# Turning the expert loop of a perceiver and mixture-of-experts block: which blocks the loop holds, and what stands behind it

## The chip, the cores and the metric

The kernel runs on one core of a Trainium2 chip. The metric is the device time of one execution in microseconds (us), the median of several runs. A profile is taken of one execution by the hardware profiler. Its times start at the first instruction.

## What is computed

The reference is one layer of three parts, each added to its input, on x of 8 x 64 rows of 512 numbers in float32: cross-attention of the normalised rows over a context of 1601 rows, linear attention with a feed-forward part, and a mixture of experts. The change touches the last alone:

```python
router_logits = x @ w_router                     # 512 rows, 8 experts
top_w, top_i = jax.lax.top_k(router_logits, 2)
top_w = jax.nn.softmax(top_w, axis=-1)
for ei in range(8):
    hmid = jax.nn.silu(x @ w0[ei]) * (x @ w1[ei])     # 512 -> 1024
    out = out + gating[:, ei:ei + 1] * (hmid @ wo[ei])
```

## The kernel before

Every engine has its own program, written out by hand, and they meet at semaphores. The work up to the router is unrolled. The experts are worked off in blocks of sorted rows. An expert with more rows than the 128 of its long block has *short blocks* of 32 rows ahead of it (`short_block`); each expert then has one *long block* of 128 rows (`expert_block`). How many short blocks an expert has is only known when the router has run. VectorE works the numbers out into a small integer tensor `blocks`, which holds for each expert the number of its first block and that of its long one, and every engine reads them into registers with a `value_load` (`expert_blocks`), two for each expert. A `Fori` with these bounds inside an `If` (for there may be no short block) runs the short blocks.

The outer `Fori` runs over experts 0 to 6 and holds the short blocks and the long block of one expert. Expert 7's long block differs (nothing follows it, and it takes part in the final sum), so the code of expert 7, short loop and long block, stands a second time behind the loop.

In a long block TensorE multiplies the gathered rows by the four halves of w0 and w1 (`up`, units 0 to 3, into banks 0 to 3), turns the product of silu and gate (`hidden_transposed`), and multiplies by the two halves of wo (`down_part`, units 4 and 5). Weights are split in two parts, so each product is three matmuls (L1532, L1535, L1536 in `product`). ScalarE copies the high part of the next expert's weights (`split_e`, L777), VectorE subtracts for the low part (L1271). A short block uses the weights unsplit (`strips`, L2013). SP's queue loads the weights of expert e + 1 (L450): unit 0 waits for `raw_free`, which TensorE's first matmul of the long block of e gives, and SP's round begins behind the store of the long block before (L469), which waits for the copy of y (`yb`, L843 on ScalarE). ScalarE's queue fetches the rows of the block after next (L812).

The order of blocks in time is set by the data alone; within a block it is the order of the code, engine by engine.

Of the kernel before, what the change touches and what calls it, by code (L numbers as in the profile page):

```python
# [5 lines left out]
def perceiver_block(nc, ins, out):  # L6
# [22 lines left out]
    E, _, FE = ins["L0_ffn_w0"].shape  # L29
    R = 32  # L30
    OV = 24
    NB = E + OV
# [11 lines left out]
    with ExitStack() as ctx:  # L44
        def sb(name, shape, dt=f32, scope=ctx):
            return scope.enter_context(nc.sbuf_tensor(name, shape, dt))
# [142 lines left out]
        blocks = sb("blocks", [P, 2, E], mybir.dt.int32, moe)  # L189
# [134 lines left out]

        def expert_blocks(engine, e):

            most = NB - 1 if isinstance(e, int) else NB - 2
            return [engine.value_load(blocks[0:1, i, bass.ds(e, 1)], min_val=0, max_val=most) for i in range(2)]

        TB = [bank[0], bank[1], bank[2]]  # L330
        SB = [bank[3], bank[4]]
# [245 lines left out]
        def _(act):  # L577
# [249 lines left out]
            def silu(b, half, n=512):  # L827
                act.wait_ge(unit_done[2 * half], b + 1)
                nc.scalar.activation(sg[half][:, 0:n], bank[2 * half][:, 0:n], ACT.Silu).then_inc(silu_ready, 1)
# [15 lines left out]
            def short_block(b):  # L845

                silu(b, 0, P)
                silu(b, 1, P)
                whole_hidden(b, 0)
                next_rows(b)  # L850
                whole_hidden(b, 1)
                output_copied(b, P)
                act.wait_ge(y_ready, b + 2)
                row = row_of(b) * R
                nc.scalar.dma_start(ys[bass.ds(row, R), :].rearrange("t (q c) -> q t c", q=FULL_R), yb[:, 0:P]).then_inc(y_stored, 16)

            def expert_block(b, e, last=False):

                def split(j):
                    if not last:  # L860
                        split_e(e + 1, j, (unit_done[j], b + 1))

                silu(b, 0)
                if last:
                    act.wait_ge(xg_loaded, 16 * b + 16)
                    act.wait_ge(y_stored, 16 * b + 1)
                    nc.scalar.activation(drained[:, :], mhalf[:, :], ACT.Copy).then_inc(prior_stored, 1)
                split_e(e, 4)
                split_e(e, 5)
                split(0)  # L870
                silu(b, 1)
                upper_hidden(b, 0)
                split(1)
                split(2)
                upper_hidden(b, 1)
                if last:
                    act.wait_ge(rank_done, 3)
                    nc.scalar.activation(in_lastT, bank[7][:, :].rearrange("p (t n) -> p t n", n=P), ACT.Copy).then_inc(gap_exp, 1)
                    act.wait_ge(unit_done[5], b + 1)
                    nc.scalar.activation(y_hi, bank[6][:, :], ACT.Copy).then_inc(y_hi_ready, 1)  # L880
                    return
                next_rows(b)
                split(3)
                output_copied(b, D)
# [4 lines left out]
                first_upper_rows(k)  # L889
            nc.scalar.activation(drained[:, :], mhalf[:, 0:NT], ACT.Silu)  # L890
            act.wait_ge(slots_ready, 5)
            with act.Fori(0, E - 1) as e:
                first_b, last_b = expert_blocks(act, e)
                with act.If(first_b < last_b):
                    with act.Fori(first_b, last_b) as b:
                        short_block(b)
                expert_block(last_b, e)
            first_b, last_b = expert_blocks(act, E - 1)
            with act.If(first_b < last_b):
                with act.Fori(first_b, last_b) as b:  # L900
                    short_block(b)
            expert_block(last_b, E - 1, last=True)

        @block.vector
        def _(dve):
# [111 lines left out]
            last = statistics((2,))  # L1017
# [257 lines left out]
            for n in range(FF // P):  # L1275
# [12 lines left out]
                if n in (1, 2):  # L1288
                    for t in range(NT):
                        last = nc.vector.tensor_tensor(xt[:, t, :], xt[:, t, :], x1n[:, t, :] if n == 1 else b2_bc, ALU.add)  # L1290
# [170 lines left out]
            def short_block(b):  # L1461

                hidden(b, 0, P)
                hidden(b, 1, P)
                lower_rows(b + 1)

            def expert_block(b, e, last=False):

                def split(j):
                    if not last:  # L1470
                        split_e(e + 1, j)

                split_e(e, 2)
                split_e(e, 3)
                hidden(b, 0)
                if last:
                    for t in range(NT):
                        half = nc.vector.tensor_scalar(in_last[:, t, :], lane[:, :], rel[0][:, t:t + 1], None, ALU.is_equal)
                    link(half)
                    for t in range(NT):  # L1480
                        whole = nc.vector.scalar_tensor_tensor(in_last[:, t, :], lane[:, :], rel[1][:, t:t + 1], in_last[:, t, :],
                                                               ALU.is_equal, ALU.add)
                    whole.then_inc(chosen_ready, 1)
                split_e(e, 4)
                split_e(e, 5)
                lower_hidden(b, 0)
                if last:
                    gates_made()
                hidden(b, 1)
                if last:  # L1490
                    gathered_added(0)
                split(0)
                lower_hidden(b, 1)
                if last:
                    return
                lower_rows(b + 1)
                split(1)

            link(nc.vector.tensor_scalar(rel_all[:, :, :], slotf_all[:, :, :], last_start[:, 0:1], None, ALU.add))
            dve.wait_ge(slots_ready, 4)  # L1500
            with dve.Fori(0, E - 1) as e:
                first_b, last_b = expert_blocks(dve, e)
                with dve.If(first_b < last_b):
                    with dve.Fori(first_b, last_b) as b:
                        short_block(b)
                expert_block(last_b, e)
            first_b, last_b = expert_blocks(dve, E - 1)
            with dve.If(first_b < last_b):
                with dve.Fori(first_b, last_b) as b:
                    short_block(b)  # L1510
            expert_block(last_b, E - 1, last=True)

            def last_added(t):

# [12 lines left out]
        def _(pe):  # L1527
# [505 lines left out]
            def short_block(b, e):  # L2033

                pe.wait_ge(xgT_lo_ready, b + KD)
                for j in range(3):
                    short_up(e, j)
                short_transposed(b, 0)
                short_up(e, 3)
                rows_transposed(b + 1)  # L2040
                short_transposed(b, 1)
                pe.wait_ge(y_ready, b + 1)
                short_down(b, e, 0)
                short_down(b, e, 1)

            def expert_block(b, e, last=False):

                pe.wait_ge(xgT_lo_ready, b + KD)
                for j in range(3):
                    up(e, j)  # L2050
                hidden_transposed(b, 0)
                up(e, 3)
                pe.wait_ge(y_ready, b + 1)
                down_ready(b, e, 0)
                down_part(0, [0])
                hidden_transposed(b, 1)
                if last:
                    pe.wait_ge(chosen_ready, NT + 1)
                    for t in range(NT):
                        mm = nc.tensor.transpose(bank[7][:, t * P:(t + 1) * P], in_last[:, t, :], ident[:, :])  # L2060
                    mm.then_inc(rank_done, 1)
                else:
                    rows_transposed(b + 1)
                down_part(0, [1, 2, 3]).then_inc(unit_done[4], 1)
                down_ready(b, e, 1)
                down_part(1, [0, 1, 2, 3]).then_inc(unit_done[5], 1)

            pe.wait_ge(slots_ready, 4)
            with pe.Fori(0, E - 1) as e:
                first_b, last_b = expert_blocks(pe, e)  # L2070
                with pe.If(first_b < last_b):
                    with pe.Fori(first_b, last_b) as b:
                        short_block(b, e)
                expert_block(last_b, e)
            first_b, last_b = expert_blocks(pe, E - 1)
            with pe.If(first_b < last_b):
                with pe.Fori(first_b, last_b) as b:
                    short_block(b, E - 1)
            expert_block(last_b, E - 1, last=True)
            pe.wait_ge(gap_exp, 2)  # L2080
            pe.wait_ge(y_lo_ready, 1)
            for t in range(NT):
# [20 lines left out]
```

## Time and profile before

| | us |
|---|---|
| median of 3 runs | 662.53 (661.16 to 662.87) |
| profiled execution | 661.3 |
| its span, first to last instruction | 659.5 |
| TensorE busy in it | 620.6 |
| VectorE, ScalarE, GpSimd busy | 429.6, 369.9, 206.7 |
| experts, first block to end of last | 438 to 650 |

The profiled execution is compared with the median with its own time, 661.3, not with its span. Busy times are sums over instructions; register, branch and load instructions of a queue count as none of it and are found by their source line (engine names with a q, as PEldq for TensorE's queue). A matmul's listed duration overlaps the next one's, so the pitch of a row of matmuls is read from their starts.

### The profile page before, as it was taken

The numbers are of one execution on the slowest core, as the hardware profiler recorded it, in microseconds if no ns is written. First come the engines' busy times: TensorE is split into PE (matmuls) and PEld (weight loads), VectorE is DVE, ScalarE is ACT, GpSimd is POOL, SyncE is SP. The second block draws the span as 40 slices with busy tenths as digits, with TensorE's granted clock in tenths as the row PEclk, the third lists the DMA queues.
The fourth block names the chain that finished last, engine by engine and source line by source line (L and its number), as shares of the span: only waits on it lengthen the run. The fifth ranks groups of instructions, "written<-read, shape, count | busy, mean of one in ns | idle before, by whom it ended". The sixth has DMA issues, their size and how long they took to land.

```text
span 659.5 us, 12277 instructions
## 1 busy us (share of the span) xinstructions
PE 620.6 (94%) x4593; PEld 503.2 (76%) x4594; DVE 429.6 (65%) x726; ACT 369.9 (56%) x556; POOL 206.7 (31%) x162
## 2 busy tenths in 40 slices
PE   8989999999989999979999999979998999999686
PEld 7867888888867888857788888867776777777464
DVE  7775766657677355666876335746951859768856
ACT  4589998979964344430152224236762747767531
POOL 4159986978893033341000000450000000000023
PEclk9999999999999999999999999979999999999897
DMA  8515544443132612299993232036971969969805
GB/s 322 220 65 199 201 146 151 168 145 128 40 121 82 194 64 96 67 362 393 401 330 108 73 118 65 0 145 237 337 278 39 330 212 339 380 234 336 295 18 173
DMA packets 56576, 125.54 MB, mean 190 GB/s; under 512 B 5200, under 2 KB 5968, under 8 KB 53464
## 3 DMA queue, kind: packets, MB, share of 16 engines
q1 hardware_dynamic: 52592, 117.00, 49.6%
q0 software_dynamic: 1280, 4.20, 1.9%
q10 hardware_dynamic: 2664, 3.80, 1.8%
q8 instruction: 26, 0.43, 0.3%
q14 instruction: 14, 0.11, 0.1%
HBM read 102.83 MB, written 22.15 MB: 190 GB/s over the span
## 4 chain that ended last, share of the span: by engine, by line
PE 71%; DMA 6%; ACT 6%; DVE 5%; issue 5%; POOL 4%; ACTq 2%; SPq 1%; POOLq 0%; DVEq 0%
PE bank L1532 15%; PE bank L1536 14%; PE bank L1535 14%; PE bank L1548 5%; DMA w_raw<-in_L_ffn_w_dram 4%; PE bank L2013 4%; PE bank L1599 3%; POOL nat_lo L505 3%; PE bank L1600 2%; PE bank L1567 2%; PE bank L1568 2%; ACT nat_hi L620 1%; POOL yt L573 1%; PE bank L1775 1%; PE bank L1584 1%
## 5 line engine op out<-in xcount | busy, mean ns | idle before, releaser
L505 POOL TENSOR_TENSOR nat_lo<-raw,nat_hi 128x512 fp32r<-128x512 f32 x104 | 136.2, 1343 | 41.9 <-ACT nat_hi L620 41.7
L925 DVE TENSOR_TENSOR ct_lo<-bank,ct_hi 128x512 fp32r<-128x512 f32 x96 | 65.9, 689 | 33.3 <-ACT ct_hi L587 32.6
L573 POOL DMA_INDIRECT yt<-slots_y,slot_all x8 | 9.4, 1170 | 200.4 <-DVE e_lo L1271 198.2
L620 ACT ACTIVATE nat_hi<-raw 128x512 fp32r<-128x512 f32 x104 | 64.7, 631 | 0.0
L587 ACT ACTIVATE ct_hi<-bank 128x512 fp32r<-128x512 f32 x96 | 57.0, 596 | 9.0 <-PE bank L1548 6.8
L1548 PE MATMUL bank<-ident,raw 128*128 128x128 f32 x384 | 57.7, 273 | 0.3
L1548 PEld LDWEIGHTS bank<-ident,raw 128*128 128x128 f32 x384 | 46.7, 140 | 12.8 <-issue 0.9
L1532 PE MATMUL bank<-w_hi,turned 128*128 128x512 f32 x128 | 51.7, 404 | 4.7 <-issue 4.6
L1532 PE MATMUL bank<-turned,w_hi 128*128 128x512 f32 (+1 forms) x144 | 53.3, 370 | 1.4 <-DVE turned L1076 1.4
L1271 DVE TENSOR_TENSOR e_lo<-e_raw,e_hi 128x2048 fp32r<-128x2048 f32 x24 | 54.1, 2284 | 0.0
L1536 PE MATMUL bank<-turned,w_lo 128*128 128x512 f32 (+1 forms) x144 | 52.8, 367 | 0.0
L1271 DVE TENSOR_TENSOR w_lo<-w_raw,w_hi 128x2048 fp32r<-128x2048 f32 (+1 forms) x24 | 52.3, 2195 | 0.7 <-ACT w_hi L777 0.7
L1535 PE MATMUL bank<-turned,w_hi 128*128 128x512 f32 (+1 forms) x144 | 52.7, 366 | 0.0
L1438 DVE TENSOR_TENSOR hm<-bank,vectors 128x512 f32<-128x512 f32 (+1 forms) x28 | 14.6, 520 | 57.5 <-PE bank L1536 25.7
L1536 PE MATMUL bank<-w_hi,turned 128*128 128x512 f32 x128 | 50.6, 396 | 0.0
L1535 PE MATMUL bank<-w_lo,turned 128*128 128x512 f32 x128 | 50.6, 396 | 0.0
L1599 PE MATMUL bank<-nat_hi,pT 128*128 128x512 f32 x104 | 48.6, 467 | 1.6 <-POOL nat_lo L505 1.1
L777 ACT ACTIVATE w_hi<-w_raw 128x2048 fp32r<-128x2048 f32 x24 | 45.7, 1917 | 4.3 <-DMA w_raw<-in_L_ffn_w_dram 4.3
L777 ACT ACTIVATE e_hi<-e_raw 128x2048 fp32r<-128x2048 f32 x24 | 45.1, 1913 | 1.2 <-issue 1.2
L527 POOL TENSOR_TENSOR w_lo<-w_raw,w_hi 128x2048 fp32r<-128x2048 f32 x6 | 27.6, 4604 | 56.1 <-ACT w_hi L674 56.1
L1532 PE MATMUL bank<-e_hi,turned 128*128 128x512 f32 x96 | 40.9, 426 | 4.2 <-DVE turned L1442 4.1
L1600 PE MATMUL bank<-nat_lo,pT 128*128 128x512 f32 x104 | 40.9, 393 | 0.0
(292 smaller groups left out, 1448.9 us busy)
## 6 DMA issues: line engine op xcount, KB each, us to landing
raw<-in_ctx_dram SPq DMA_DIRECT2D x24, 1024.0 KB, 4.9
w_raw<-in_L_ffn_w_dram SPq DMA_DIRECT2D x24, 1024.0 KB, 7.7
e_raw<-in_L_ffn_wo_dram SPq DMA_DIRECT2D x16, 1024.0 KB, 9.4
w_raw<-in_L_attn_w_dram SPq DMA_DIRECT2D x8, 1024.0 KB, 5.9
slots_x<-zeros SPq DMA_DIRECT2D x1, 8192.0 KB, 28.0
slots_y<-zeros SPq DMA_DIRECT2D x1, 8192.0 KB, 32.9
e_raw<-in_L_ffn_w_dram SPq DMA_DIRECT2D x8, 1024.0 KB, 11.4
vectors<-slots_x ACTq DMA_DIRECT2D x13, 256.0 KB, 5.6
```

What stands on the lines that cost most here:

```text
L505: nc.gpsimd.tensor_tensor(nat_lo[:, j, :], raw[b % 2][:, j, :], nat_hi[:, j, :].bitcast(f32), ALU.subtract).then_inc(nat_lo_ready, 1)
L587: nc.scalar.activation(ct_hi[:, n % CR, :], src, ACT.Copy).then_inc(t_hi, 1)
L620: nc.scalar.activation(nat_hi[:, j, :], raw[b % 2][:, j, :], ACT.Copy).then_inc(nat_hi_ready, 1)
L777: nc.scalar.activation(e_hi[j][:, :, :], e_raw[j][:, :, :], ACT.Copy).then_inc(e_hi_ready[j], 1)
L925: nc.vector.tensor_tensor(ct_lo[:, n % CR, :], src, ct_hi[:, n % CR, :].bitcast(f32), ALU.subtract).then_inc(t_lo, 1)
L1271: low = nc.vector.tensor_tensor(e_lo[j][:, rows_, :], e_raw[j][:, rows_, :], e_hi[j][:, rows_, :].bitcast(f32), ALU.subtract)
L1532: mm = nc.tensor.matmul(dst, lh, rh, start=first and k == 0, stop=False)
L1535: nc.tensor.matmul(dst, lh, rl, start=False, stop=False)
L1536: mm = nc.tensor.matmul(dst, ll, rh, start=False, stop=last and k == n - 1)
L1548: mm = nc.tensor.transpose(TB[n % 3][:, i * P:(i + 1) * P], raw[b % 2][:, CH * (g // CH) + i, (g % CH) * P:(g % CH + 1) * P], ident[:, :])
L1599: nc.tensor.matmul(value_bank(b)[:, :], pT[:, j, :], nat_hi[:, j, :], start=j == 0, stop=False)
L1600: nc.tensor.matmul(value_bank(b)[:, :], pT[:, j, :], nat_lo[:, j, :], start=False, stop=j == NKT - 1).then_inc(v_step, 1)
```

## The change

The outer loop now holds the long block of expert e and then the short blocks of expert e + 1. The short blocks of expert 0 stand ahead of the loop, and expert 7's long block stands directly behind it. The same is done on ScalarE, VectorE and TensorE; SP's loop is as before. The numbers of the short blocks' bounds are still loaded by `expert_blocks` (two loads), the number of the long block by the new `full_block` (one load), so there are three loads in a round instead of two. The diff is shown for TensorE; ScalarE's and VectorE's read the same.

```diff
@@
         def expert_blocks(engine, e):
 
+            return [engine.value_load(blocks[0:1, i, bass.ds(e, 1)], min_val=0, max_val=NB - 1) for i in range(2)]
+
+        def full_block(engine, e):
+
             most = NB - 1 if isinstance(e, int) else NB - 2
-            return [engine.value_load(blocks[0:1, i, bass.ds(e, 1)], min_val=0, max_val=most) for i in range(2)]
+            return engine.value_load(blocks[0:1, 1, bass.ds(e, 1)], min_val=0, max_val=most)
@@
             pe.wait_ge(slots_ready, 4)
+            first_b, last_b = expert_blocks(pe, 0)
+            with pe.If(first_b < last_b):
+                with pe.Fori(first_b, last_b) as b:
+                    short_block(b, 0)
             with pe.Fori(0, E - 1) as e:
-                first_b, last_b = expert_blocks(pe, e)
+                expert_block(full_block(pe, e), e)
+                first_b, last_b = expert_blocks(pe, e + 1)
                 with pe.If(first_b < last_b):
                     with pe.Fori(first_b, last_b) as b:
-                        short_block(b, e)
-                expert_block(last_b, e)
-            first_b, last_b = expert_blocks(pe, E - 1)
-            with pe.If(first_b < last_b):
-                with pe.Fori(first_b, last_b) as b:
-                    short_block(b, E - 1)
-            expert_block(last_b, E - 1, last=True)
+                        short_block(b, e + 1)
+            expert_block(full_block(pe, E - 1), E - 1, last=True)
```

What follows are rows of the program in the order in which it stands, not in which it runs; a taken branch leaves them. First TensorE before, from the last matmuls in the loop to the first of the last block (L2069 is the outer loop, L328 the loads, L2076 and L2077 the If and the inner loop; L2013 are matmuls of short blocks, of which there are more rows than the first shown).

```order
L1535 MATMUL bank<-e_lo,turned 128x512
L1536 MATMUL bank<-e_hi,turned 128x512
L2069 REGISTER_ALU
L2069 COMPARE_AND_BRANCH
L328 TENSOR_LOAD blocks
L328 ISA x2
L328 TENSOR_LOAD blocks
L328 ISA x2
L2076 COMPARE_AND_BRANCH
L2077 UNCONDITIONAL_BRANCH
L2077 ISA
L2013 MATMUL bank<-w_raw,in_last 32x128 x48
```

The same place of TensorE after, the end of a long block, which is now in the middle of the loop (L327 the two loads of `expert_blocks`, L2080 and L2081 the If and the inner loop).

```order
L1539 MATMUL bank<-e_lo,turned 128x512
L1540 MATMUL bank<-e_hi,turned 128x512
L327 ISA
L327 TENSOR_LOAD blocks
L327 ISA x3
L327 TENSOR_LOAD blocks
L327 ISA x2
L2080 COMPARE_AND_BRANCH
L2081 UNCONDITIONAL_BRANCH
L2081 ISA
L2024 REGISTER_ALU
L2017 MATMUL bank<-w_raw,in_last 32x128 x32
```

So the outer loop's branch no longer stands between a long block and the If behind it; the If and the short block's code follow the same matmuls in both. Next TensorE between the end of a short block's code in the loop and the long block behind it, before.

```order
L2013 MATMUL bank<-e_raw,in_last 32x128 x32
L2072 REGISTER_ALU
L2072 COMPARE_AND_BRANCH
L2071 UNCONDITIONAL_BRANCH
L2048 REGISTER_ALU
L1990 REGISTER_ALU
L1532 MATMUL bank<-w_hi,turned 128x512
```

And after, where the outer loop (L2077) turns behind the short blocks; what stands below its branch is the last block of expert 7, and the loop's start has the same load (L332, `full_block`) ahead of its long block.

```order
L2017 MATMUL bank<-e_raw,in_last 32x128 x32
L2081 REGISTER_ALU
L2081 COMPARE_AND_BRANCH
L2080 UNCONDITIONAL_BRANCH
L2077 REGISTER_ALU
L2077 COMPARE_AND_BRANCH
L332 TENSOR_LOAD blocks
L332 ISA x2
L2052 REGISTER_ALU
L1536 MATMUL bank<-w_hi,turned 128x512
```

Between a short block and a long one there now stand the outer loop's branch and one load; behind the loop no short block is left.

## Rows read from the trace of the kernel before

**Rows 1.** The page: busy share of TensorE; instruction packets of its queue, count and MB.

```profile
PE 620.6 (94%) x4593; PEld 503.2 (76%) x4594; DVE 429.6 (65%) x726; ACT 369.9 (56%) x556; POOL 206.7 (31%) x162
...
q8 instruction: 26, 0.43, 0.3%
```

**Rows 2.** Busy time by stretch, experts; (x) counts instructions.

```profile
core 0: us, PE busy (x) PEld busy (x) DVE busy (x) ACT busy (x) POOL busy (x), PEclk, DMA share, GB/s
...
468.00:488.00 20.00, 19.15 (x95) 14.80 (x97) 16.79 (x12) 14.36 (x13) 0.00 (x0) 1.00 0.94 345
...
512.00:530.00 18.00, 18.00 (x83) 14.36 (x84) 14.88 (x11) 13.95 (x13) 0.00 (x0) 1.00 0.92 341
530.00:538.00 8.00, 7.55 (x201) 6.00 (x200) 2.72 (x4) 2.49 (x8) 0.00 (x0) 1.00 0.38 126
```

**Rows 3.** The chain of waits, 600 to 626: start, us, what.

```profile
603.57 0.45 SPq L450
...
604.27 9.91 DMA w_raw<-in_L_ffn_w_dram
```

**Rows 4.** Timeline of TensorE, 483 to 489.

```profile
484.86 0.48 PE L1532 MATMUL bank<-e_hi,turned 128*128 128x512 f32 x1 [0.85 <-DVE turned L1442]
```

**Rows 5.** Timeline of TensorE at the loop's exit, 620 to 630.5.

```profile
620.11 0.40 PE L1536 MATMUL bank<-e_hi,turned 128*128 128x512 f32 x1
625.10 0.77 PE L1532 MATMUL bank<-w_hi,turned 128*128 128x512 f32 x1 [4.59 <-issue]
...
629.49 0.40 PE L1535 MATMUL bank<-w_lo,turned 128*128 128x512 f32 x1
629.72 0.40 PE L1536 MATMUL bank<-w_hi,turned 128*128 128x512 f32 x1
```

**Rows 6.** Source line L2076: ns minimum/median/maximum, first and last start.

```profile
L2076 PEldq COMPARE_BRANCH  x1: 5722/5722/5722, 619.1 to 619.1; - x1
```

**Rows 7.** Source line L2071, the If in the loop.

```profile
L2071 PEldq COMPARE_BRANCH  x7: 80/105/218, 437.5 to 600.1; - x7
```

**Rows 8.** DMA queues, 622.3 to 623.6.

```profile
q8 instruction: 1, 0.02, 5.3%
```

**Rows 9.** DMA queues, 444.9 to 446.

```profile
q8 instruction: 1, 0.02, 5.2%
```

**Rows 10.** DMA queues, 450.6 to 452.

```profile
q8 instruction: 1, 0.02, 4.3%
```

**Rows 11.** DMA queues, 452 to 622, the whole list.

```profile
q1 hardware_dynamic: 23006, 45.56, 72.8%
q10 hardware_dynamic: 2520, 3.54, 6.5%
q14 instruction: 2, 0.02, 0.0%
```

**Rows 12.** Busy time by stretch at the exit; the third figure from the end is TensorE's granted clock.

```profile
620.50:622.60 2.10, 0.01 (x1) 0.00 (x0) 2.10 (x2) 0.60 (x1) 0.00 (x0) 1.00 0.87 313
622.60:629.50 6.90, 4.40 (x11) 3.48 (x12) 1.98 (x1) 0.00 (x0) 0.00 (x0) 0.51 0.07 25
```

**Rows 13.** Timeline of VectorE, 617 to 633.

```profile
622.30 2.28 DVE L1271 TENSOR_TENSOR e_lo<-e_raw,e_hi 128x2048 fp32r<-128x2048 f32 x1
632.91 0.69 DVE L1438 TENSOR_TENSOR hm<-bank,vectors 128x512 f32<-128x512 f32 x1 [8.32 <-PE bank L1536]
```

**Rows 14.** Source line L328, the loads, 485.2 to 487.

```profile
L328 PEldq TENSOR_LOAD <-blocks x2: 300/304/307, 485.4 to 486.2; - x2
```

**Rows 15.** Source line L2069, the outer loop's branch, 484 to 486.5.

```profile
L2069 PEldq COMPARE_BRANCH  x1: 217/217/217, 485.0 to 485.0; - x1
L2069 PEldq FUSED_REGOPS  x1: 50/50/50, 485.3 to 485.3; - x1
```

**Rows 16.** Source line L2072, the inner loop's branch, 510 to 512.5.

```profile
L2072 PEldq COMPARE_BRANCH  x1: 76/76/76, 511.2 to 511.2; - x1
```

**Rows 17.** Timeline of TensorE's weight loads, 511.4 to 512.

```profile
511.87 0.19 PEld L1532 LDWEIGHTS bank<-w_hi,turned 128*128 128x128 f32 x1 [0.20 <-issue]
```

More of the change, by code:

```diff
@@ L891, in _ @@
             act.wait_ge(slots_ready, 5)
+            first_b, last_b = expert_blocks(act, 0)
+            with act.If(first_b < last_b):
+                with act.Fori(first_b, last_b) as b:
+                    short_block(b)
             with act.Fori(0, E - 1) as e:
-                first_b, last_b = expert_blocks(act, e)
+                expert_block(full_block(act, e), e)
+                first_b, last_b = expert_blocks(act, e + 1)
                 with act.If(first_b < last_b):
@@ L896, in _ @@
                         short_block(b)
-                expert_block(last_b, e)
[L898 to L901, printed above, removed]
-            expert_block(last_b, E - 1, last=True)
+            expert_block(full_block(act, E - 1), E - 1, last=True)
         @block.vector
@@ L1500, in _ @@
             dve.wait_ge(slots_ready, 4)
+            first_b, last_b = expert_blocks(dve, 0)
+            with dve.If(first_b < last_b):
+                with dve.Fori(first_b, last_b) as b:
+                    short_block(b)
             with dve.Fori(0, E - 1) as e:
-                first_b, last_b = expert_blocks(dve, e)
+                expert_block(full_block(dve, e), e)
+                first_b, last_b = expert_blocks(dve, e + 1)
                 with dve.If(first_b < last_b):
@@ L1505, in _ @@
                         short_block(b)
[L1506 to L1511, printed above, removed]
+            expert_block(full_block(dve, E - 1), E - 1, last=True)
             def last_added(t):
@@ L2068, in _ @@
             pe.wait_ge(slots_ready, 4)
+            first_b, last_b = expert_blocks(pe, 0)
+            with pe.If(first_b < last_b):
+                with pe.Fori(first_b, last_b) as b:
+                    short_block(b, 0)
             with pe.Fori(0, E - 1) as e:
-                first_b, last_b = expert_blocks(pe, e)
+                expert_block(full_block(pe, e), e)
+                first_b, last_b = expert_blocks(pe, e + 1)
                 with pe.If(first_b < last_b):
                     with pe.Fori(first_b, last_b) as b:
-                        short_block(b, e)
-                expert_block(last_b, e)
-            first_b, last_b = expert_blocks(pe, E - 1)
-            with pe.If(first_b < last_b):
-                with pe.Fori(first_b, last_b) as b:
-                    short_block(b, E - 1)
-            expert_block(last_b, E - 1, last=True)
+                        short_block(b, e + 1)
+            expert_block(full_block(pe, E - 1), E - 1, last=True)
             pe.wait_ge(gap_exp, 2)
```

## The prediction

> **What bounds the kernel now.** I read first the page: TensorE is busy for 620.6 of 659.5 us, no other engine for more than 430 [rows 1]. Then a table of the expert part by stretch, to see whether that also holds there. It does: in the long blocks that follow a short one (450 to 468, 512 to 530, 538 to 556) TensorE is busy 18.0 of 18 us, with some 84 matmuls, and a short block is some 200 matmuls in 8 us [rows 2]. So whatever makes TensorE late there is paid in full. The table also shows the order of the blocks, which the data fix: expert 0 has one short block, 1 none, 2 three, 3 one, 4 none, 5 one, 6 and 7 none.
>
> Two places are not full. Ahead of the long blocks of experts 2 and 3 nothing is lost, but the long blocks that follow a long one directly (468 to 488, 556 to 575, 601 to 620.5) take 0.6 to 0.85 us more. The chain of waits runs there through the copy of y, SP's issue and a weight transfer of 9.9 us [rows 3], and TensorE stands 0.85 us in the first of them [rows 4]. The other place is the way out of the loop. The last matmul of expert 6 starts at 620.11, the first of the last block at 625.10, with 4.59 us idle that no engine released [rows 5]. The queue's own rows say what it did: the branch of the If at L2076, which jumps over the static copy of the short block, began at 619.1 and took 5.72 us [rows 6], where the If in the loop takes 0.08 to 0.22 [rows 7]. Inside those 5.72 us an instruction packet of the 16 KB kind was moved, between 622.3 and 623.6 [rows 8]. So this is code that was not there when it was jumped to.
>
> When is code fetched otherwise? 26 such packets carry TensorE's program [rows 1]. The run executed 4593 matmuls with as many weight loads; without the repeats of the loop (five short blocks of some 400 instructions, six long ones of 168) and with the short copy that never ran this leaves about 6,580 different ones, an estimate of 253 in a packet. One was moved at 444.9 to 446, in the middle of the first short block, and the next at 450.6 to 452, just as the first long block had begun [rows 9, 10]: about 253 instructions apart, so a packet comes each time TensorE's queue walks over a boundary, and it is the one after that in which it now is. From 452 to 622 none came, only two of the other engines' small ones [rows 11]: the loop's 600 instructions stay. At 450.7 the queue had therefore a boundary just behind it: its own packet held the long block and the loop's end, the packet ahead the first 253 instructions after that, and the last block starts some 590 after the start of the long one, in the third packet. That is why the jump missed.
>
> **The change, part by part.** In code order nothing moves: before it is short, long, short, long with the first pair as the loop, after it is the same four pieces with the middle pair as the loop. The matmuls, copies, transfers and their order in time are the same on every engine. Three things change: which jumps are taken, how many values are loaded per round (three instead of two), and where the loop turns.
>
> *(a) The last block.* It now stands right behind the loop's end, and TensorE's queue gets there by the loop's own tail. If that code is there, the 4.59 us go. With them goes what the clock lost: the granted clock was 0.51 from 622.6 to 629.5, where the stretch before shows 1.00 [rows 12], so the ten matmuls from 625.10 to 629.49 took 4.39 us where ten at full clock take 2.33 (0.23 each) [rows 5], a loss of 2.06 us. VectorE was ready: its weight splits ended at 624.6 and it then waited 8.32 us for TensorE [rows 13], so all behind it moves along. Sum: -6.65 us.
>
> *(b) The jump over the short block, now inside the loop.* After the long block of expert 0 come two loads and the If; expert 1 has no short block, so the branch jumps over the block's 400 instructions to the loop's end. That is the same jump as the one at L2076 before, from the same place in the code to the same place, and it is taken at 467 with the packet of 450.6 as the last one fetched [rows 10]. I expect the same miss there. It costs the 4.59 us, plus what now stands behind the branch and not ahead of it: the loop's branch (from 485.0 to 485.3, 0.3) [rows 15] and one load. The loop's two loads start at 485.4 and 486.2, 0.76 us apart with their address and check [rows 14]. That gives 5.6 us idle. The clock: it fell 2.1 us after TensorE stopped and stayed down 6.9 [rows 12]; with 1.1 us more of standing still, 3.4 us are run at half speed, a loss of 1.6. Against it, the 0.85 us of waiting in this block [rows 4] vanish, since the transfers are released by TensorE's start while the clock slows only TensorE. Sum: +6.35 us.
>
> *(c) The third load at other turns.* It is free where TensorE's own queued matmuls cover it. After a short block they do not: the inner branch is decided at 511.2, the next weight load starts at 511.87, and it takes only 0.3 us of queue work to get there [rows 16, 17]. After the change the loop's branch (0.3) and a load (0.76), followed by two register operations (0.2), stand between: the weight load comes at 512.64, 0.77 us late. Three times (experts 2, 3, 5): 2.3 us. Expert 0's long block is entered from above, a load without a taken branch: 0.5 us. The first loads of all have no loop set-up in front: -0.2. At the skips ahead of experts 4 and 6 the next block may start up to 0.76 late, but these are the blocks whose end the weight transfer decides, and that starts from the y copy, not from TensorE [rows 3]; their 0.6 to 0.85 us of waiting cover it: 0. At the exit the third load leaves about 0.1. If the cover were gone, 1.5 more. Sum: +2.7 us.
>
> On ScalarE, VectorE and SP the added load is 0.65 to 0.8 us, ahead of work that waits for TensorE anyhow (VectorE 8.32 us at the extreme [rows 13]): 0. Their short blocks are three operations on VectorE and nine on ScalarE, so no jump of theirs goes far.
>
> Sum: -6.65 + 6.35 + 2.7 = +2.4 us on the profiled execution's 661.3 (span 659.5 and 1.8 around it), 663.7. The median of the runs is 662.5 (661.2 to 662.9), 1.2 higher, so I say **665.0 us**.
>
> Bounds of what the trace doesn't show: from the packet's start at 622.3 to the first matmul at 625.10 lie 2.8 us that any miss has; the 3.2 from the branch to the packet may be shorter where the transfers leave room. They left little at the exit (share 0.87 at 620.5 to 622.6 [rows 12]), and the jump at 467 falls in a stretch with 0.94 [rows 2], so I take the whole 4.59; 1.8 less if not. The clock's loss lies between 0 (no fall) and 2.1; (c) between 1.0 and 4.2. Together: 661 to 668.
>
> The Trainium skill has a rule against this change, in "Runtime: NRT & Kernel Launch", section "Instruction fetch mechanics": a taken branch whose target is outside the current two pages of instructions forces a fetch, and there is no cache beyond them. This trace has the forced fetch, and contradicts the two pages: the loop's 600 instructions are more than two packets of 253 and turned six times without a fetch [rows 11]. By the page the loop after, which also touches the jump's target, would fetch at every round; the same page gives TensorE room for 2048 instructions, by which it would not. No row here holds more than four packets at once.
>
> **The rivals.**
> 1. *The target is there: no miss in the loop.* For it: the packet ahead could be the right one if the boundary lay later than I count. Against: the target is 400 instructions on, more than one packet, and the jump over the same distance missed [rows 6]. Time: 662.5 - 6.65 + 2.7 = 658.6 us. This ends on the other side. It decides itself by one thing: whether the packet that holds the loop's tail is moved by TensorE's walk before 467.
> 2. *The back jump misses too.* A forced fetch may drop what was held, and the loop's start, which lies close to a boundary by the time of its packet [rows 10], would be fetched anew. Nothing in the trace before speaks to it, since it never jumps back after a miss. Another 4.6 to 5.7 us: 670.
> 3. *The loop no longer fits.* It now touches four packets and the one ahead. If four is the limit, each of seven rounds pays at least 4.6 us: 695 or more. For it: no row shows five held. Against: nothing shows a limit either. The two-page rule of the Trainium skill named above is this rival.
> 4. *All hidden.* The load's 0.77 us after short blocks vanish in some slack and the miss is a us or two shorter, while the transfers are less crowded: 661 to 663.
>
> **How the numbers follow.** Moved stall as summed 0.66 (own range 662.5 to 668); rival 4 0.12; rivals 1, 2 and 3 0.08, 0.08, 0.06. The likeliest is 665.0. The range 661.0 to 670.5 leaves out rivals 1 and 3 and the tails. A measurement of this kernel tells 0.3%, 2.0 us, from no change; the sum of 2.4 is close to that, so of the 0.66 I give a third part below it or just at it: slower 0.57, same 0.32, faster 0.11.
>
> **What the profile after would show.** The branch of the If in TensorE's loop with a longest time of some 5.7 us, at 467; an instruction packet at about 470.5 and one at 473.5, and none at 622; TensorE idle 5.6 us at 468.8 without a releaser, and at 620 less than 0.3. The granted clock at half around 471 to 478. Long blocks after short ones starting 0.7 to 0.8 us after the last short matmul's usual gap. I am wrong if the idle time at 468.8 is missing (rival 1), if a second one follows it directly (rival 2) or returns at each round (rival 3), and wrong in (c) if the long blocks after short ones start without delay.

## The result: 0.36% slower, 664.4 us

20 runs of each on the same chips: the changed kernel 664.38 us in the median (662.90 to 666.20, and one execution of 868.8 at a granted clock of 0.65, which the ratio leaves out), the kernel before 662.49 (660.07 to 664.19). The ratio is 1.0036, with a 95% interval of 1.0026 to 1.0046: 2.4 us slower (662.5 x 0.0036), between 1.7 and 3.0. The profiled execution has a span of 663.2 us where before it had 659.5.

The page of the changed kernel has the same work and the same 26 instruction packets as before [rows 1]:

```profile
PE 621.0 (94%) x4593; PEld 503.4 (76%) x4594; DVE 429.8 (65%) x726; ACT 370.0 (56%) x556; POOL 207.1 (31%) x162
...
q8 instruction: 26, 0.43, 0.2%
```

The If over the short block is now L2080, inside TensorE's loop (duration in ns, shortest, middle and longest; first and last start). Before, its longest time was 218 ns [rows 7] and the one outside the loop took 5722 [rows 6]. Its first execution is the long one:

```profile
L2080 PEldq COMPARE_BRANCH  x7: 80/212/4217, 468.5 to 629.1; - x7
```

The timeline of TensorE shows both places. The idle time of 4.29 us stands behind expert 0's long block, and at the loop's exit, where 4.59 us stood [rows 5], nothing is left:

```profile
469.54 0.40 PE L1540 MATMUL bank<-e_hi,turned 128*128 128x512 f32 x1
474.22 0.79 PE L1536 MATMUL bank<-w_hi,turned 128*128 128x512 f32 x1 [4.29 <-issue]
...
630.17 0.40 PE L1540 MATMUL bank<-e_hi,turned 128*128 128x512 f32 x1
630.49 0.47 PE L1536 MATMUL bank<-w_hi,turned 128*128 128x512 f32 x1
```

The DMA queues between 470 and 471.6 hold one of TensorE's 16 KB packets, and so do those between 473.4 and 474.8; from 475 to the end of the loop and beyond, to 662, the whole list has none (q8 is missing):

```profile
q8 instruction: 1, 0.02, 4.3%
...
q1 hardware_dynamic: 20384, 40.27, 59.1%
q10 hardware_dynamic: 2244, 3.21, 5.6%
q0 software_dynamic: 640, 2.10, 3.9%
```

By stretch (length, TensorE's busy time, then granted clock, DMA share, GB/s), the clock falls behind the idle time as it did at the old exit [rows 12]: it is still at 2.4 GHz from 472.0 to 473.4, with TensorE idle, and at 1.2 from 473.4 to 480.2. The 14 matmuls in that stretch would take 3.2 us at full clock (0.23 each), so 2.8 us are lost:

```profile
472.00:473.40 1.40, 0.00 (x0) 0.99 0.31 116
473.40:480.20 6.80, 5.98 (x14) 0.50 0.56 188
480.20:488.00 7.80, 7.80 (x37) 1.00 1.05 387
```

The third load, together with the loop's branch at the same place, shows in the chain of waits (start, us, what): at each of the three long blocks that follow a short one in the loop there is now a piece that no engine released, where the chain of before shows from 446 to 635 only one such piece among its longest, the 4.59 us at the exit:

```profile
469.94 4.29 issue
...
519.59 0.72 issue
...
546.23 0.76 issue
...
591.93 0.76 issue
```

Two profiles give 3.7 us of difference where the medians give 1.9. Where the rest comes from can be read: from the start of expert 0's long block to the end it is 209.68 us before (449.86 to 659.54) and 212.38 after (450.82 to 663.2), 2.70 apart. Of the 1.0 us that arose earlier, 0.56 is the third load ahead of that block (term c below), and the rest lies in the first short block and ahead of it, where profiles differ (last section). So the change's own part of these two profiles is some 3.3 us, an estimate from them that lies just above the interval of 1.7 to 3.0 (part of it is how long the clock stayed low in this one profile, see term b).

### The profile page after: what moved, and what is told of

Same layout as the page of the kernel before. It is cut to its first block, busy times and chain, and to the rows that moved or that the text cites. A ratio compares the mean times of both kernels' runs of the same rounds, so it can differ in the third digit from the quotient of the medians.

```text
span 663.2 us, 12368 instructions
## 1 busy us (share of the span) xinstructions
PE 621.0 (94%) x4593; PEld 503.4 (76%) x4594; DVE 429.8 (65%) x726; ACT 370.0 (56%) x556; POOL 207.1 (31%) x162
## 4 chain that ended last, share of the span: by engine, by line
PE 74%; DVE 6%; issue 5%; ACT 5%; DMA 4%; POOL 4%; ACTq 2%; SPq 1%; POOLq 0%; DVEq 0%
PE bank L1536 16%; PE bank L1540 15%; PE bank L1539 15%; PE bank L1552 5%; PE bank L2017 4%; DMA w_raw<-in_L_ffn_w_dram 3%; PE bank L1603 3%; POOL nat_lo L509 3%; PE bank L1604 2%; PE bank L1571 2%; PE bank L1572 2%; ACT nat_hi L624 1%; POOL yt L577 1%; PE bank L1779 1%; PE bank L1588 1%
```

## The experiments

Each was timed against the kernel before on the same chip; a ratio holds its 95% interval. The first four were run together, with 660.97 us for the kernel before, the next three with 662.39, and the last with 661.50.

### The exit's jump taken away

```diff
             first_b, last_b = expert_blocks(pe, E - 1)
-            with pe.If(first_b < last_b):
-                with pe.Fori(first_b, last_b) as b:
-                    short_block(b, E - 1)
             expert_block(last_b, E - 1, last=True)
```

> The kernel before, with TensorE's static copy of expert 7's short block left out; expert 7 has no short block in this data, so nothing that was executed is missing. Theory (the idle ahead of the last long block is code fetched for the jump over that copy, and the half clock follows from the idle): both go, 4.59 + 2.06 = 6.65 us, median 662.5 - 6.65 = 655.9 us; TensorE's gap ahead of the last block 0.2 to 0.5 us, the branch there under 0.3 us, no q8 packet near it. Rival A (the gap is the loads and the branch themselves, whatever code stands between): gap and median stay, 662.5 us. Rival B (the idle was covered: what it delays waits for the expert's weights anyway): the gap becomes a wait for weights or VectorE, 660 to 662.5 us.

Measured: 654.79 us, ratio 0.9892 (0.9864 to 0.9920), 7.1 us less (5.3 to 9.0). The timeline of TensorE at the exit, with the first matmul of the last block 0.23 us behind its predecessor:

```profile
618.95 0.40 PE L1536 MATMUL bank<-e_hi,turned 128*128 128x512 f32 x1
619.18 0.40 PE L1532 MATMUL bank<-w_hi,turned 128*128 128x512 f32 x1
```

The idle time and the half clock that followed it belong to the jump over code that was never run. Both rivals fall: the two loads are still there and cost nothing, and nothing else was covered by the gap.

### The third load alone, and the change without it

The kernel before with a load more, on TensorE, VectorE and ScalarE alike:

```diff
-                expert_block(last_b, e)
+                expert_block(full_block(pe, e), e)
```

> The kernel before, with the long block's number read once more ahead of each long block of the loop, on TensorE, VectorE and ScalarE: the change's third load alone, with the blocks where they were. Theory: 0.77 us at the long blocks behind a short one (experts 2, 3, 5), 0.5 at expert 0's, and the same on experts 1, 4, 6 only as far as their weights are not waited for: 2.8 to 3.1 us, median about 665.4 us; the LDWEIGHTS gap ahead of those blocks 0.31 + 0.5 to 0.8 us. Rival (a load on the queue is hidden behind the block before, and what the traces showed came from the new order of code): median 662.5 to 663 us, gaps of 0.31 us unchanged.

Measured: 663.61 us against 660.97, ratio 1.0018 (0.9995 to 1.0042), 1.2 us, less than half of what I expected, though the interval reaches up to 2.8. The trace decides: the weight load ahead of expert 2's long block comes after 0.52 us (TensorE's weight loads), where it came after 0.20 before [rows 17]:

```profile
514.34 0.19 PEld L1536 LDWEIGHTS bank<-w_hi,turned 128*128 128x128 f32 x1 [0.52 <-issue]
```

That is 0.3 us for a load that takes 0.65 on the queue. At experts 0, 3 and 5 it is the same (0.33, 0.28 and 0.31 us more from weight load to weight load than before), 1.2 us in all, which is also the difference of the times.

The changed kernel with the number kept in a register instead of loaded:

```diff
                 first_b, last_b = expert_blocks(pe, e + 1)
+                keep(pe, last_b)
...
-            return engine.value_load(blocks[0:1, 1, bass.ds(e, 1)], min_val=0, max_val=most)
+            return engine.snap(kept[engine], min_val=0, max_val=most)
...
+        def keep(engine, last_b):
+            engine.reg_mov(kept[engine], last_b)
```

> The changed kernel without its third load: the long block's number is kept in a register of each engine across the loop's end, and read from there. Theory (the third load costs 0.5 to 0.83 us at each long block that isn't covered by a wait): 2.7 to 3.3 us less than the changed kernel, median 661.1 to 661.7 us; gaps ahead of long blocks back at 0.3 us; the miss at 468.5 stays at 4 us. Rival (the gaps come from the loop's own branches, which now lie between a short block and its long one): median 664.4 us, gaps of 0.8 to 1.1 us stay.

Measured: 660.85 us, ratio 0.9988 (0.9968 to 1.0007), which is 0.48% or 3.2 us less than the changed kernel's 1.0036 (1.7 to 4.7, from both intervals). The same weight load, with the loop's end still between the blocks:

```profile
515.55 0.19 PEld L1548 LDWEIGHTS bank<-w_hi,turned 128*128 128x128 f32 x1 [0.22 <-issue]
```

So the loop's end alone costs 0.02 us there, the load alone 0.32, and both together, in the changed kernel, 0.78:

```profile
520.30 0.19 PEld L1536 LDWEIGHTS bank<-w_hi,turned 128*128 128x128 f32 x1 [0.98 <-issue]
```

The records of TensorE's queue in the four traces give the reason. From the start of the inner branch (511.2 before) to that of the last register operation ahead of the weight load (511.4) the queue takes 0.23 us before, 0.61 with the loop's end, 0.91 with the load and 1.37 with both: 0.38, 0.68 and 1.14 us more. The weight load came 0.02, 0.32 and 0.78 us later. The difference is 0.36 us each time: by so much the queue is ahead at the end of a short block, and only what goes beyond it is paid. What one addition costs thus depends on the others at the same place. The miss is not touched by this: its branch took 4.5 us, as expected.

### The fetch brought forward

A hint for the coming branch, one instruction at the head of TensorE's loop in the changed kernel; the If is written as a branch, so that the hint can name it:

```diff
             with pe.Fori(0, E - 1) as e:
+                ahead = nc.mark_branch_hint_location(mybir.EngineType.PE)
                 expert_block(full_block(pe, e), e)
                 first_b, last_b = expert_blocks(pe, e + 1)
-                with pe.If(first_b < last_b):
+                pe.br_lt(first_b, last_b, on_true="pe_short", on_false="pe_no_short").branch_hint(ahead)
...
```

> The changed kernel, with one instruction more at the head of TensorE's loop: a branch prefetch hint for the branch that jumps over the short block. Theory (the 4.29 us idle at 469.5 is the fetch of the code behind the short block, not held when expert 1 skips it): a hint in time makes the packet come before the jump, the branch takes under 0.3 us, and idle and half clock go, 4.29 + 2.8, less 0.85 for the wait that returns: about 6.2 us, median 664.4 - 6.2 = 658.2 us. Rival A (the hint does nothing, or the idle isn't a fetch): branch of 4 us stays, 664.4 us. Rival B (the hint takes the place of the next packet in order, so expert 2's short block, the first that is walked into, misses instead): the idle moves to about 488 us, 663 to 665 us.

Measured: 663.19 us, ratio 1.0022 (1.0001 to 1.0043). Against the changed kernel's 1.0036 that is 0.9 us less, with intervals that overlap, and not the 6.2 of the theory. The trace says why; it is rival B. The branch now takes 0.4 us at most:

```profile
L2082 PEldq COMPARE_BRANCH  x7: 84/227/397, 468.6 to 627.1; - x7
```

and TensorE is idle for 0.58 us instead of 4.29, with the clock at 1.00 behind it. But expert 2's short block, the first in the loop that runs, then stalls in its first matmuls (timeline of TensorE), and a 16 KB packet moves at 490 to 491:

```profile
470.55 0.49 PE L1536 MATMUL bank<-w_hi,turned 128*128 128x512 f32 x1 [0.58 <-issue]
...
493.15 0.71 PE L2017 MATMUL bank<-w_raw,in_last 128*32 128x128 f32 x17 [2.16 <-issue]
```

In both kernels one packet moves between 456 and 457. I conclude, from the order of the packets and not from their contents, that in the changed kernel it held the short block's middle, and with the hint the branch's target, so that the middle is missing when it is needed. The starts of the blocks, against the changed kernel, give the account: expert 1's 3.7 us earlier (470.55 against 474.21), expert 2's short 6.0 earlier (489.47 against 495.47), its long block 3.0 (517.28 against 520.30), and 2.0 at the last (628.45 against 630.46). So 3.0 us went in expert 2's short blocks, with the moved miss, and 1.0 in the rounds after, where the gap ahead of expert 2's long block is 1.36 us from weight load to weight load and 1.09 without the hint. The page of this run counts 28 packets where both other kernels have 26; besides the one at 490 to 491, one moves between 494.8 and 496 and one between 508.3 and 509.5, without idle time at either:

```profile
q8 instruction: 28, 0.46, 0.3%
```

This shows that the 4.29 us are a fetch. It does not give the size of one without other traffic: the stretch of the idle time has a DMA share of 0.41, with the clock unmoved, but the one just before it 0.94, and the queue may have asked for the packet while TensorE still worked:

```profile
490.20:490.90 0.70, 0.70 (x31) 1.00 0.94 334
490.90:493.20 2.30, 0.14 (x7) 0.05 (x7) 0.00 (x0) 0.28 (x1) 0.00 (x0) 1.00 0.41 148
```

### One engine's part at a time

The change on TensorE alone, with VectorE and ScalarE as before:

```diff
-            with pe.Fori(0, E - 1) as e:
-                first_b, last_b = expert_blocks(pe, e)
...
+            with pe.Fori(0, E - 1) as e:
+                expert_block(full_block(pe, e), e)
+                first_b, last_b = both_blocks(pe, e + 1)
...
             with dve.Fori(0, E - 1) as e:
                 first_b, last_b = expert_blocks(dve, e)
```

and the other way round for the second; both_blocks is the change's pair of loads under another name.

> The change on TensorE alone; VectorE and ScalarE keep the old order, with two loads for each expert. Theory (all of the change's terms lie on TensorE): the same as the whole change, 1.0036 times before, with the branch of 4 to 5.7 us at 468 and LDWEIGHTS gaps of 0.8 to 1.1 us. Rival (a good part of the cost of the third load is VectorE's, whose halves turned later hold TensorE): 1 us or more below the whole change.

> The change on VectorE and ScalarE alone; TensorE keeps the old order. Theory: no difference, the branch of 5.7 us at the exit stays, median within 0.15% of before. Rival (VectorE's third load counts): 1 us or more above before.

Measured: 1.0024 (1.0002 to 1.0047) for TensorE alone, with the branch of 4.25 us at 469.8 and the pieces of 0.76 us in the chain; 0.9997 (0.9974 to 1.0019) for the other two, with the branch of 5.8 us at the exit. The traces put the change's terms on TensorE; the times agree, but their intervals are too wide to exclude some tenths of a per cent from VectorE or ScalarE.

### One loop over all experts

The theory says which order should have no miss at all: every stretch is walked through once before it is jumped over, and the last block begins next to walked code. TensorE's part of the edit (VectorE's and ScalarE's read the same, and `last_block` loads the number once more):

```diff
-            with pe.Fori(0, E - 1) as e:
+            with pe.Fori(0, E) as e:
                 first_b, last_b = expert_blocks(pe, e)
                 with pe.If(first_b < last_b):
                     with pe.Fori(first_b, last_b) as b:
                         short_block(b, e)
-                expert_block(last_b, e)
-            first_b, last_b = expert_blocks(pe, E - 1)
-            with pe.If(first_b < last_b):
-                with pe.Fori(first_b, last_b) as b:
-                    short_block(b, E - 1)
-            expert_block(last_b, E - 1, last=True)
+                with pe.If(e < E - 1):
+                    expert_block(last_b, e)
+            expert_block(last_block(pe), E - 1, last=True)
```

> One loop over all eight experts on TensorE, VectorE and ScalarE: short blocks, then the long block for experts 0 to 6 only; expert 7's long block stands directly behind the loop and reads its number once more. Nothing of the work is left out. Theory (a jump stalls when it goes to code that has not been held yet, and only then): in this order expert 0 walks through the short and the long block before either is jumped over, and the last block begins in code next to what was walked, so no branch takes over 0.5 us, neither at 468 nor at the exit: -6.65 against before, +0.1 to +0.3 at each of the eight blocks for the branch that is new between short and long: 654.5 to 656.5 us if before is at 661.0. Rival (leaving the loop over the long block stalls again, since the last block's code wasn't walked): the branch of 4 to 6 us stays, 661 to 663 us.

Measured: 655.26 us against 662.39, ratio 0.9909 (0.9880 to 0.9937), 6.0 us less than before (4.2 to 7.9). The two Ifs and the exit on TensorE's queue, none over 0.23 us, and the DMA queues from 454 to 622 without a packet of TensorE's:

```profile
L2069 PEldq COMPARE_BRANCH  x8: 86/155/224, 437.6 to 621.9; - x8
L2072 PEldq COMPARE_BRANCH  x8: 70/74/202, 450.3 to 622.2; - x8
...
q1 hardware_dynamic: 22678, 44.91, 73.6%
q10 hardware_dynamic: 2432, 3.39, 6.4%
q14 instruction: 1, 0.01, 0.0%
```

The branch that is new between short and long costs nothing: the gap between the weight loads is 0.31 us there at experts 2, 3 and 5, as before, and only at expert 0 more (0.56); my 0.1 to 0.3 for each block was too much. At the exit, where two jumps, the loop's end and a load come together, 0.64 us of idle remain in the chain of waits:

```profile
622.96 0.64 issue
```

The same with the last number kept in a register:

```diff
                 first_b, last_b = expert_blocks(pe, e)
+                keep(pe, last_b)
...
-            return engine.value_load(blocks[0:1, 1, E - 1:E], min_val=0, max_val=NB - 1)
+            return engine.snap(kept[engine], min_val=0, max_val=NB - 1)
```

> The one-loop order, with the last long block's number kept in a register of each engine instead of loaded again behind the loop. Theory (a load and a loop's end are each nearly hidden by TensorE's queue, and stall it only when they come together): the LDWEIGHTS gap ahead of the last block falls from 1.23 to between 0.3 and 0.6 us, no other gap grows by over 0.05 us, 0.6 to 0.9 us less than the one-loop order: ratio to before 0.988 to 0.991. Rival (the gap of 1.23 us is code that comes late, a short miss): it stays over 1 us, the ratio stays 0.991.

Measured: ratio 0.9908 (0.9878 to 0.9937). The gap from weight load to weight load ahead of the last block fell from 1.23 to 0.62 us, just above the 0.3 to 0.6 that I expected, and the idle piece left the chain: the gap was queue work, not a late fetch. The time can't tell 0.6 us, and the saving of 0.6 to 0.9 us that I expected doesn't show in it. One other gap, ahead of expert 1's block, grew from 0.23 to 0.36, more than the 0.05 that I allowed; why wasn't tried.

## Why the prediction was right, and where it wasn't

It said 665.0 us, and slower by 2.4 us on the profiled execution; the ratio gives 2.4 (1.7 to 3.0). The mechanism is the predicted one; that the two parts of (b) erred by nearly the same amount in opposite ways is luck. Term by term:

**(a), -6.65 us: right.** The idle time at the exit is gone in the trace after, and removing the jump alone gave -7.1 (5.3 to 9.0). The gap ahead of the last block is 0.52 us from weight load to weight load, where 0.23 is usual between two long blocks: 0.3 for the load, of which I had put 0.1.

**(b), +6.35 us: right in its sum, and its parts erred both ways.** I expected a branch of 5.7 us and 5.6 idle; it took 4.22 and 4.29. The step that failed is taking the whole delay from branch to packet (3.2 us at the old exit) because the stretch had a DMA share of 0.94: the packet came 1.7 us after the branch, which began at 468.5. My lower bound, 1.8 us less, is near that number, but not its condition, "where the transfers leave room". They left none: until shortly before the packet the share was 1.03, as it was at the old exit (1.04), where the packet took 1.5 us longer to come (before first, then after; length, TensorE's busy time, clock, share, GB/s):

```profile
619.10:621.40 2.30, 1.41 (x7) 1.00 1.04 386
621.40:622.40 1.00, 0.00 (x0) 1.00 0.70 246
...
468.50:469.90 1.40, 1.40 (x7) 1.00 1.03 382
469.90:470.20 0.30, 0.04 (x1) 1.00 0.92 335
470.20:471.20 1.00, 0.00 (x0) 1.00 0.37 121
```

In both, the packet comes as the transfers in progress run out. The other traces with a miss agree. In the loop the packet came 1.8 us (the change on TensorE alone) and 2.0 us (the number in a register) behind the branch, at the exit 3.2 us (the load alone) and 3.4 us (the other two engines), and from the packet's start to the end of the branch it is 2.5 us in all six. So the delay ahead of the packet goes by how long the transfers under way still last, as far as six traces tell, and not by the share; no run varied it on purpose.

The clock's loss went the other way, 2.8 us for my 1.6: the low clock began 3.5 us after TensorE stood still and not 2.1, and lasted 6.8 us, so most of it fell on running matmuls. That is this profile's, not the change's: with the change on TensorE alone, with the same miss, the low clock lasted 3.4 us, and its eight matmuls lost 1.4:

```profile
475.40:478.80 3.40, 3.24 (x8) 0.50 0.30 46
```

The wait of 0.85 us [rows 4] vanished as foreseen. From the start of expert 0's long block to that of expert 2's short one the trace after takes 6.67 us more (44.65 against 37.98): 4.67 in the gap (4.90 us from weight load to weight load for 0.23), 1.60 in expert 1's block, and 0.4 at a wait in expert 0's block that before doesn't have and I hadn't foreseen:

```profile
466.89 0.47 PE L1536 MATMUL bank<-e_hi,turned 128*128 128x512 f32 x1 [0.34 <-DVE turned L1446]
```

In the profile with the change on TensorE alone the same stretch took 43.24 us, 5.3 more than before. (b) thus lies between 5.3 and 6.7 by two profiles, and 6.35 is within.

**(c), +2.7 us: right in size, half right in its reason.** Measured ahead of the long blocks of experts 0, 2, 3 and 5: +0.56, +0.78, +0.82 and +0.82 us (predicted 0.5 and three times 0.77), 3.0 in all. The delays at the skips, 0.53 and 0.49, were covered, as I said. In expert 4's block the wait for VectorE was 0.61 us before and is gone after. In expert 6's it is still there, 0.44 us for 0.75:

```profile
617.48 0.47 PE L1532 MATMUL bank<-e_hi,turned 128*128 128x512 f32 x1 [0.75 <-DVE turned L1442]
...
627.52 0.47 PE L1536 MATMUL bank<-e_hi,turned 128*128 128x512 f32 x1 [0.44 <-DVE turned L1446]
```

But I said that TensorE's queued matmuls cover nothing after a short block, and my own rows say otherwise: 0.67 us lie between the inner branch and the weight load for 0.3 of queue work. The sum used these 0.3 to 0.4 us (1.06 us of work were added, 0.77 came out) without naming them, and called all that was left the third load; my expectation of 0.77 us for the load alone comes from there. Alone, the load costs 0.32, the loop's end 0.02. Dropping the load gave back 3.2 us (1.7 to 4.7), which fits the whole of (c), since the loop's end then hides.

**The rivals.** Rival 1 (the target is there) is refuted by the branch of 4.22 us. It can be had, though: the one-loop order is that case, and better than I gave for it, as it needs no third load in the loop. Rival 3 (a miss at every round) is refuted by the list of queues from 475 to 662, which holds no packet. For rival 2 (the jump back misses too) the packet between 473.4 and 474.8 has to be told apart, since the jump back began at 472.9. It was not its fetch: the branch took 0.26 us, a second packet follows the first by the same 3.2 us before, where nothing jumps back (622.4 and 625.6), and both kernels move 26, so none came twice.

```profile
L2077 PEldq COMPARE_BRANCH  x1: 258/258/258, 472.9 to 472.9; - x1
```

Between 444.5 and 474.6 four packets came that the loop and the stretch behind it use, with the one in which the loop starts, that makes five by this count, and six more rounds ran from them. This is against the two pages in the Trainium skill, "Runtime: NRT & Kernel Launch", "Instruction fetch mechanics", for TensorE; its other statement there, that a taken branch to a target outside of that window waits for a fetch, agrees with the 4.22 us only as to a target that isn't held. Rival 4 (all hidden, 661 to 663) is right in that the miss was shorter, by 1.5 us of branch, and that the load alone is half hidden; with the loop's end ahead of it the delay is whole, and the median is 664.4.

The bounds of the prediction taken together give 660 to 667 (1.8, 1.6 and 1.7 below 665.0, 0.5 and 1.5 above) and not 661 to 668; nothing else hangs on it.

## What to carry to other kernels

A rarely taken piece of code that is jumped over costs a fetch at the first jump, and turning the loop only moves the jump: look in the trace for a branch of several us on the engine's queue and an instruction packet inside it. Order the code so that the data's first rounds walk through each piece before they skip it; here that gave 0.9% (0.6 to 1.2) with no computation changed. Price added register work on a queue together with all that stands at the same place, since only what exceeds the queue's lead is paid.

## What the runs showed of the hardware

- A miss took 4.2, 4.25, 4.5, 5.7, 5.7 and 5.8 us of branch. The last 2.5 us of each, from the packet's start on, are the same; what differs is the 1.7 to 3.4 us until the packet comes, which it does as the weight transfers under way run out. Behind all six the granted clock fell to 0.5, for 3.4 or 6.8 us. With the hint the idle time was 2.16 us, and the clock stayed.
- A prefetch hint works on TensorE (branch 0.4 us for 4.2), but the miss moved to the code that was walked into next, and 28 packets moved instead of 26: as I read this run, the hinted packet took the place of the next one in order rather than adding to it.
- Single profiles differ in one place that none of the edits touches, the gather of rows within expert 0's short block. TensorE shows no wait for it in the two profiles of the change, before and after, and up to 4.45 us elsewhere. Two kernels with the same instructions there waited 1.59 us (the first, without the exit's jump) and 3.89 (the second, the change on TensorE alone), by their timelines:

```profile
444.81 0.66 PE L1983 MATMUL bank<-ident,vectors 128*128 128x128 f32 x4 [1.59 <-DMA vectors<-slots_x]
```

```profile
447.58 1.11 PE L1992 MATMUL bank<-ident,vectors 128*128 128x128 f32 x4 [3.89 <-DMA vectors<-slots_x]
```

Why it varies wasn't tried. A comparison of two traces is better begun behind it, at expert 0's long block, as above.
